# Last layer of a four-layer convolution kernel: tap rows stacked in one product and gathered two chunks later, silu loads moved to GpSimd's queue, distance kept in a buffer of its own, ScalarE's squares put first in each unit

## What the reference computes

```python
patches = _extract_patches(x, KSIZE, STRIDE, PAD)      # 3x3 taps, zero padded
bspl = _b_splines(patches, grid)                       # 8 cubic B-splines of each value
base_w = base_weight.sum(axis=2)
spl_w = (spline_weight * spline_scaler[..., None]).sum(axis=2)
out = jnp.einsum('bjhwn,ijn->bihw', jax.nn.silu(patches), base_w)
out = out + jnp.einsum('bjhwns,ijns->bihw', bspl, spl_w)
out = out + bias_weight[None, :, None, None]
```

## Time and profile before

| | |
|---|---|
| median of three runs | 12108.91 us |
| the profiled execution's own time | 12114.81 us |
| its span | 12112.6 us |
| busy, whole span | PE 79%, DVE 74%, ACT 61%, POOL 42%, weight loads 36% |
| stretch up to the last layer | 0 to 11147 us |
| last layer, loading and norm | 11147 to 11295 us: PE busy 1.14 us, DMA share 0.72 |
| last layer, main loop | 11295 to 12112.6 us: PE 756.88 us, DVE 600.97, ACT 394.12, POOL 307.99 of 817.6; clock 0.96, DMA share 0.45 |

### The profile page before, as it was taken

The page is one execution under the profiler, slowest core; times in us unless marked ns, Lnnn a source line. Parts: engine busy times, 40 slices in busy tenths (PEclk is TensorE's granted clock), DMA queues, the critical chain, the costliest instruction groups (busy, mean ns, idle before and its releaser), DMA issues. The chain is left out here.

```text
span 12112.6 us, 205123 instructions
## 1 busy us (share of the span) xinstructions
PE 9570.5 (79%) x53055; PEld 4412.5 (36%) x53055; DVE 8958.4 (74%) x10913; ACT 7397.5 (61%) x10963; POOL 5088.7 (42%) x2442
## 2 busy tenths in 40 slices
PE   0788578857886788640199999999999999997599
PEld 0566456645664566510022222222222222222233
DVE  1778487847784787637488888888888888887677
ACT  0455345534553455324288888888888888886354
POOL 0233133312321233100166666666666666665243
PEclk9899789977997799875599999999999999999799
DMA  2000100010000000004311111111111111112544
GB/s 86 1 0 0 28 8 0 0 29 7 0 0 21 15 0 0 37 28 143 98 29 29 29 27 25 28 29 29 29 29 29 29 29 27 28 26 54 130 115 100
DMA packets 227136, 410.60 MB, mean 34 GB/s; under 512 B 28784, under 2 KB 163024, under 8 KB 212336
## 3 DMA queue, kind: packets, MB, share of 16 engines
q1 hardware_dynamic: 226150, 399.26, 12.9%
HBM read 283.44 MB, written 115.70 MB: 33 GB/s over the span
## 5 line engine op out<-in xcount | busy, mean ns | idle before, releaser
L1194 POOL TENSOR_TENSOR l_a<-l_a 128x1018 f32<-128x1018 f32 x1851 | 3453.3, 1883 | 1687.8 <-ACT l_a L1339 1673.0
L1309 DVE TENSOR_TENSOR l_r<-l_pps,l_a 128x509 f32<-128x509 f32 x4755 | 2989.0, 677 | 46.0 <-PE l_pps L1208 28.1
L1333 ACT ACTIVATE l_a<-l_qps 128x509 f32<-128x509 f32 x3705 | 2155.3, 596 | 818.4 <-PE l_qps L1208 566.0
L1339 ACT ACTIVATE l_a<-l_a 128x1018 f32<-128x1018 f32 x2380 | 2504.0, 1052 | 40.3 <-issue 40.3
L1208 PE MATMUL l_qps<-l_mv,l_wst 123*128 123x509 bf16 x4235 | 1644.6, 388 | 170.1 <-ACT l_a L1333 50.0
L1208 PE MATMUL l_pps<-l_mv,l_wst 123*128 123x509 bf16 x4228 | 1624.4, 384 | 63.6 <-DVE l_r L1309 60.9
L652 POOL TENSOR_TENSOR a_pr<-a_pr 128x768 f32<-128x768 f32 x384 | 898.4, 2340 | 1639.1 <-DVE a_pr L567 1624.0
L681 ACT ACTIVATE a_g<-a_fps 128x512 f32<-128x512 f32 x1152 | 680.4, 597 | 998.7 <-PE a_fps L434 997.3
L434 PE MATMUL a_fps<-a_hbt,a_wfc 96*128 96x512 f32 x2304 | 1222.2, 666 | 70.2 <-ACT a_g L681 70.2
L452 POOL TENSOR_TENSOR a_pr<-a_qkv 128x768 f32<-128x768 f32 x128 | 386.6, 3039 | 2089.3 <-ACT a_qkv L694 2089.3
L1297 DVE TENSOR_SCALAR l_a<-l_qps 128x509 int32<-128x509 int32 x1058 | 724.5, 685 | 688.2 <-PE l_qps L1208 677.6
(11 more groups left out here) (162 smaller groups left out, 12030.2 us busy)
## 6 DMA issues: line engine op xcount, KB each, us to landing
l_mv<-pw SPq DMA_DIRECT2D x1608, 79.5 KB
l_gx<-g SPq DMA_DIRECT2D x66, 1040.0 KB
pw<-pw_hi SPq DMA_DIRECT2D x165, 127.2 KB
pw<-pw_mid SPq DMA_DIRECT2D x165, 127.2 KB
pw<-pw_lo SPq DMA_DIRECT2D x165, 127.2 KB
a_tb<-g SPq DMA_DIRECT2D x16, 1031.9 KB
l_x<-x SPq DMA_DIRECT2D x16, 1024.0 KB, 12.1
l_gs<-g SPq DMA_DIRECT2D x33, 260.0 KB
```

The costliest lines, as they stand in the source:

```text
L1194: g.tensor_tensor(a, a, a, ALU.mult).then_inc(sq_p, 2)
L1309: v.tensor_tensor(R[:, m % R_RING, :], pps[:, m % P_BANKS, 0:SUB], A[:, m % A_RING, :], ALU.mult).then_inc(mul_done, 1)
L1333: s_.activation(A[:, s % A_RING, :], qps[:, s % Q_BANKS, 0:SUB], ACT.Abs).then_inc(abs_a, 1)
L1339: s_.activation(a, a, ACT.Abs_reciprocal_sqrt, bias=1.0).then_inc(root_done, 2)
```

## The change

Seven things are changed in the last layer; the other layers keep their instructions.

1. The spline products of a chunk no longer read shifted rows. The weights of the three tap rows stand side by side (`wsp`: 3 x 16 columns, padded to 64), so one product gives the contributions of a pixel to three output rows at once, as three "planes". Per image and unit there are three products (the column taps), 24 in a chunk, which go to one PSUM bank per image pair (`pps`, six banks), unit 0 to partitions 0 to 63, unit 1 to 64 to 127.
2. The planes are copied from PSUM to a ring in SBUF (`planes`, three chunks), three of four by ACT and the fourth by DVE (`keep`).
3. `gather(k)` then adds, two chunks later, the planes of three neighbouring rows with 12 small products against a 0/1 matrix (`pick`).
4. The silu is stacked by two: partitions 64 to 127 of `gs` hold the rows one further down, so that one product covers tap rows 0 and 1 and a second one tap row 2. `gs` becomes one buffer of 128 x 1040, filled by six DMAs per chunk that GpSimd issues once the silu before has been taken.
5. The distance goes to a buffer `vb` instead of back to `gx`; `gx` has two buffers instead of three, and is loaded again once the distance has been taken (`v_done`).
6. The slope a is taken on ACT (a Relu, with its sign turned), and the last addition moves from POOL to DVE. POOL does no arithmetic any more.
7. ACT's order in a unit: squares first, then the next unit's distance and slope, then the copies and the silu. `a2` and `b2` have one buffer each. The load of one more small array and a few small DVE and POOL instructions are added ahead of the loop.

```diff
-GX, BSLOTS = 3, 3
+GX, BSLOTS, PSLOTS, PBANKS = 2, 2, 3, 6
+HALF = 2
+KEEP_DVE = {3}
...
                     if n >= GX:
-                        sp.wait_ge(b3_done, n - GX + 1)
+                        sp.wait_ge(v_done, n - GX + 1)
                     src = g3[k, e].rearrange("c j n -> c (j n)").unsqueeze(0).broadcast_to([SPLINE, C, UNIT])
                     sp.dma_start(gx[:, n % GX, :], src).then_inc(gx_in[n % GX], 16)
-                    if e == 0:
-                        if k >= 2:
-                            sp.wait_ge(silu_done, k - 1)
-                        sp.dma_start(gs[:, k % 2, :], g3[k].rearrange("e c j n -> j (e c) n")).then_inc(gs_in[k % 2], 16)
-                    elif k >= 4:
-                        store(k - 4)
+                    if e == 1 and k >= 6:
+                        store(k - 6)
...
+            def silu_after(n):
+                return (n - 3) // PARITY if n >= 3 and n % PARITY else None
+            def kept_after(n):
+                return ((n - 3) // PARITY, (0, 1) if n % PARITY else (2, 3)) if n >= 3 else (None, ())
+            def finished_after(n):
+                return (n - 8) // PARITY if n >= 8 and n % PARITY == 0 and (n - 8) // PARITY < NOUT else None
...
+            @block.gpsimd
+            def _(pool):
+                def load_silu(k):
+                    if k:
+                        pool.wait_ge(silu_done, k)
+                    for h in range(HALF):
+                        rows = g3[k].rearrange("e c j n -> j (e c) n")[2 * h:2 * h + 2]
+                        nc.gpsimd.dma_start(gs[0:64, h, :], rows).then_inc(gs_in, 16)
+                        nc.gpsimd.dma_start(gs[64:P, h, 0:CHN - QW], rows[:, :, QW:]).then_inc(gs_in, 16)
+                        if k + 1 < NCK:
+                            below = g3[k + 1].rearrange("e c j n -> j (e c) n")[2 * h:2 * h + 2, :, 0:QW]
+                            nc.gpsimd.dma_start(gs[64:P, h, CHN - QW:], below).then_inc(gs_in, 16)
...
                 def distance(n):
-                    x = gx[:, n % GX, :]
+                    x = vb[:, n % 2, :]
                     act.wait_ge(gx_in[n % GX], (n // GX + 1) * 16)
-                    s_.activation(x, x, ACT.Abs, bias=place[:], scale=1.0 / GRID_STEP).then_inc(v_done, 1)
+                    if n >= 2:
+                        act.wait_ge(bases, n - 1)
+                    s_.activation(x, gx[:, n % GX, :], ACT.Abs, bias=place[:], scale=1.0 / GRID_STEP).then_inc(v_done, 1)
+                    act.wait_ge(v_done, n + 1)
+                    s_.activation(na[:, n % 2, :], x, ACT.Relu, bias=two[:], scale=-1.0).then_inc(na_done, 1)
...
+                        act.wait_ge(na_done, n + 1)
+                        if n:
+                            act.wait_ge(a3_done, n)
+                        s_.activation(a2[:], na[:, n % 2, :], ACT.Square).then_inc(a2_done, 1)
+                        act.wait_ge(nb_done, n + 1)
+                        if n:
+                            act.wait_ge(b3_done, n)
+                        s_.activation(b2[:], vb[:, n % 2, :], ACT.Square, scale=2.0).then_inc(b2_done, 1)
                     if n + 1 < NUNIT:
                         distance(n + 1)
...
+                        v.tensor_tensor(x, a2[:], x, ALU.mult).then_inc(a3_done, 1)
+                        dve.wait_ge(b2_done, n + 1)
+                        v.tensor_tensor(y, b2[:], y, ALU.mult).then_inc(b3_done, 1)
+                        dve.wait_ge(a3_done, n + 1)
+                        dve.wait_ge(b3_done, n + 1)
+                        if e == 0 and k >= BSLOTS:
+                            dve.wait_ge(plane_made, (k - BSLOTS + 1) * QUAD)
+                        v.tensor_tensor(B[:, e, :, at:at + CHN], y.rearrange("p (j n) -> p j n", j=QUAD),
+                                        x.rearrange("p (j n) -> p j n", j=QUAD), ALU.add).then_inc(bases, 1)
...
+                def multiply(k):
+                    pe.wait_ge(bases, PARITY * (k + 1))
+                    at = k % BSLOTS * CHN
+                    for j in range(QUAD):
+                        m = k * QUAD + j
+                        if m >= PBANKS:
+                            wait_kept(m - PBANKS)
+                        for dx in range(3):
+                            for e in range(PARITY):
+                                x = B[:, e, j, at:at + CHN].rearrange("p (r w) -> p r w", w=QW)[:, :, dx:dx + W]
+                                last = t.matmul(pps[64 * e:64 * e + 64, m % PBANKS, :].rearrange("p (r w) -> p r w", w=W), wsp[:, dx, :],
+                                                x, start=dx == 0, stop=dx == 2, skip_group_check=True)
+                        last.then_inc(plane_made, 1)
...
+                    wait_kept((k + 2) * QUAD - 1)
                     for dy in range(3):
                         for to, n, row in pieces(k, dy):
...
+                            for j in range(QUAD):
+                                last = t.matmul(rows_out[32 * j:32 * j + 32, to:to + n, :], pick[:, dy, :],
+                                                planes[:, j, row:row + n, :], start=False, stop=dy == 2, skip_group_check=True)
                     last.then_inc(o_made, 1)
...
+                for k in range(NCK):
+                    multiply(k)
+                    if k >= 2:
+                        gather(k - 2)
+                gather(NOUT - 1)
```

More of the change, by code:

```diff
@@ new lines, in keep @@
+            def keep(e, copy, k, j):
+                e.wait_ge(plane_made, k * QUAD + j + 1)
+                if k >= PSLOTS:
+                    e.wait_ge(o_made, k - PSLOTS + 1)
+                at = k % PSLOTS * CROWS
+                return copy(planes[:, j, at:at + CROWS, :], pps[:, (k * QUAD + j) % PBANKS, :].rearrange("p (r w) -> p r w", w=W))
+            @block.gpsimd
[11 more added lines that the diff above has]
+                for k in range(NCK):
+                    load_silu(k)
@@ L1545, in _ @@
+                    for j in js:
+                        if j not in KEEP_DVE:
+                            keep(act, lambda to, of: s_.activation(to, of, ACT.Copy), k, j).then_inc(plane_kept, 1)
+                    k = silu_after(n)
+                    if k is not None:
                         silu(k)
@@ L1577, in _ @@
[L1577 to L1591, removed]
+                slope(0)
@@ new lines, in _ @@
+                for n in range(NUNIT + 7):
+                    if n < NUNIT:
+                        k, e = divmod(n, PARITY)
+                        at = k % BSLOTS * CHN
+                        x, y = na[:, n % 2, :], vb[:, n % 2, :]
+                        dve.wait_ge(a2_done, n + 1)
+                        v.tensor_tensor(x, a2[:], x, ALU.mult).then_inc(a3_done, 1)
[7 more added lines that the diff above has]
+                                        x.rearrange("p (j n) -> p j n", j=QUAD), ALU.add).then_inc(bases, 1)
+                    if n + 1 < NUNIT:
+                        slope(n + 1)
+                    k, js = kept_after(n) if n < NUNIT + 3 else (None, ())
+                    for j in js:
+                        if j in KEEP_DVE:
+                            keep(dve, v.tensor_copy, k, j).then_inc(plane_kept_v, 1)
+                    k = finished_after(n)
+                    if k is not None:
+                        finish(k)
@@ L1612, in _ @@
                     pe.wait_ge(silu_done, k + 2)
-                    silu = S[:].rearrange("p k (r w) -> p (k r) w", w=QW)
-                    first = True
+                    silu = S[:].rearrange("p k h (r w) -> p k h r w", w=QW)
+                    for both, dy in ((0, 0), (1, 2)):
+                        for to, n, row in pieces(k, dy):
+                            slots = [(to, n, row)]
+                            if row % CROWS + n > CROWS:
+                                cut = CROWS - row % CROWS
+                                slots = [(to, cut, row), (to + cut, n - cut, row + cut)]
+                            for to_, n_, row_ in slots:
+                                slot, r = divmod(row_, CROWS)
+                                for dx in range(3):
+                                    for h in range(HALF):
+                                        t.matmul(rows_out[64 * h:64 * h + 64, to_:to_ + n_, :],
+                                                 wba[:, both, dx, :, :].rearrange("p b f -> p (b f)"),
+                                                 silu[:, slot, h, r:r + n_, dx:dx + W], start=both == 0 and dx == 0, stop=False,
+                                                 skip_group_check=True)
@@ L1735, in lay_out @@
     got["w3_base"] = np.ascontiguousarray(np.broadcast_to(bw, (NB,) + bw.shape).reshape(P, 9, 9, C))
-    got["w3_mask"] = np.repeat(np.eye(NB, dtype=f32), C, axis=0)
+    got["w3_mask"] = np.tile(np.repeat(np.eye(QUAD, dtype=f32), C, axis=0), (2, 1))
+    planes = np.zeros((2, 4, C, 3, 2, C), f32)
+    for dy in range(3):
+        for e in range(2):
+            planes[e, dy, :, dy, e, :] = np.eye(C)
```

(1 more changed line is left out.)

113 lines of the change are left out of this document (48 added, 65 removed).

## The result

The changed kernel takes 12095.17 us (median of 20 runs, 12052.21 to 12115.38) against 12120.04 us (20 runs) for the one before: ratio 0.9976, 95% interval [0.9966, 0.9986]. It is faster by a quarter of a per cent. I had forecast 12005 us, about 104 us under the kernel before; 25 us came, so three quarters of the gain are missing.

What follows compares the result with a forecast made beforehand. TensorE bounded the old kernel, the loads close behind; afterwards loads bound it at 18.2 + 0.6 + 1.5 = 20.3 us a chunk. 11350.8 + 32.5 P gives 12010.5, corrected to 12005 us for the profiled run's offset; range 11940 to 12080.

Steps and rivals of the forecast that it cites:

- TensorE 18.3 us a chunk: Matrix work in the main loop: 10.4 spline, 5.3 silu, 2.6 gathering if 64-wide products pair; 5.2 us less than before.
- ScalarE 18.1: ScalarE's work in us per main-loop chunk: two units 15.3, PSUM copies 1.8, silu 1.06.
- VectorE's slope: The one slope left on VectorE per unit of the main loop takes 1.24 us.
- The waits between them: Waits among ScalarE, VectorE and TensorE in the main loop cost nothing while a chunk takes above 18 us.
- The `gx` loads as the new bound: In the main loop the loads replace TensorE as bound: 18.2 + 0.6 + 1.5 = 20.3 us a chunk; chance 0.62.
- P: Main-loop period per chunk, forecast 20.3 us; time = 11350.8 + 32.5 P; must be under 23.5 to gain anything.
- the chain of 16.8 us: Next chunk's silu loading, from GpSimd's six issues through landing to the silu: 16.8 us, hidden under 20.3.
- Rival C: Single silu buffer: GpSimd issues up to 3.07 us each make ScalarE wait at its silu; 32.7 us a chunk, 12408; chance 0.08.
- B's cost: Rival: silu loads cost the main loop's gx loads 5.0 us a chunk; 23.8 us, 12118, no change; chance 0.09.
- E: Rival: TensorE idles 2 us a main-loop chunk and its clock falls, costing 1.5 us; 19.8, under 20.3; chance 0.02 in another form.
- The last line of the prediction: Named the main way to be wrong: a silu piece on an engine also carrying gx delays the whole load.
- Faster: Whole kernel's direction: faster than before with chance 0.76, against same 0.11 and slower 0.13.

Runs made afterwards that it cites:

- nosilu: Changed kernel with the silu loads of chunks 1 to 32 left out, output not the reference's: 11953.67 us, ratio 0.9866, loop 654.0 us.
- wide16: Changed kernel with silu pieces put in channel-then-image order, so each uses 16 engines: 11983.8 us, ratio 0.9893, loop 668.1 us.
- gx16: Changed kernel with the gx load spread over 16 engines (channel-then-centre order), silu pieces unchanged: 11947.34 us, ratio 0.9856, loop 647.4 us.
- nogx: Changed kernel with gx loads left out after the first two, units computed from old data: 11964.03 us (one run), loop 653.4 us.
- both16: Changed kernel with both the silu pieces and the gx load on 16 engines: 11942.66 us, ratio 0.9852, loop 646.0 us.

## Why the prediction was wrong, step by step

- TensorE 18.3 us a chunk: right (18.32). ScalarE 18.1: right (17.87 in a chunk without waits). VectorE's slope: right. The waits between them: right; no such wait is left where the loads are out of the way (nosilu).
- The `gx` loads as the new bound: mis-sized. To the 18.2 us of two loads I added 0.6 for the store and 1.5 for the silu. Without the silu two loads and a store fit into TensorE's 18.3 us a chunk (nosilu), and with wide pieces P is 18.9, not 20.3. In the changed kernel the loads are not the bound at all.
- The step that failed: "The silu of the next chunk waits for all six, and they start only when the silu before is done: 6 x 0.6 + 12.1 (landing beside a load) + 1.1 = 16.8 us, hidden under 20.3." The issues cost 0.65 to 0.7 us, about as taken. The landing was the error: 12.1 us was that of one output store behind one load. The silu's six pieces lie on few engines each (two, by the rule in the next item) and meet loads that come without a gap. The last of them took up to 26.5 us to land, and the chain of 16.8 us took 30 in the long cases (11580.92 to 11611.12). In about every second chunk it was longer than the chunk; that is 125.7 us of waits, and P = 22.2 instead of 18.3.
- I had the rule of the two engines beside this and drew the wrong conclusion from it. The Trainium skill, DMA: Bandwidth & Descriptors, section "Why a DMA increments its semaphore by 16 and not by 1", gives two engines for a piece whose slowest dimension is 2. I used it for what the silu costs the load, not for what the load costs the silu. With the slowest dimension at 32 (wide16) or the load's at 16 (gx16) the waits were all but gone (5.1 and 3.4 us), as by that rule.
- Rival C named the place (ScalarE at its silu, behind it the squares and copies) with the wrong price: the issue, not the landing. B's cost was not found. E happened in a small way: TensorE stood idle for 2.25 us ahead of the silu's products at 11612.34, and from 11612 to 11616 its mean clock was 0.57, near the lower level of 0.50 (1.2 GHz), where the four microseconds before had 1.00. Over the whole stretch the clock was 0.93. It came after the stalls and did not set the time: TensorE waited for the splines next.
- The last line of the prediction was the mirror image of what happened: I feared that a silu piece on one of the load's engines would delay the load, and it was the load that delayed the piece.
- Faster was right as a direction; the size was not.

What stays open: the loop is 43.5 us shorter in the traces, the medians differ by 25. The profiled execution of the kernel before was 5 us under its median, and the number of long waits can differ from run to run; I did not separate these. How two queues take turns on an engine was not measured: the trace does not say on which engine a packet ran. That `gx` beside the pieces is the cause is shown (nogx, gx16), and so is that the pieces' own width matters (wide16); the turn-taking is argued. GpSimd's pauses between issues have no releaser in the trace.

## What to carry to other kernels

When a load moves to a single buffer, compare the next use with its worst landing beside the traffic that will be there, not with a median of another transfer, and count the engines it is spread over. The DMA share at 0.48 did not mean room: with one load in flight it was 0.49, half of the engines were full, and an eight-fold repeat on the outside of the access pattern was the reason. Swapping the repeat with the channels was worth 126 us of the loop here (773.8 to 647.4), but only after TensorE's work had shrunk; before that it was worth nothing.

## What the hardware showed that I had not expected

- The same 1040 KB load ran at 117 GB/s with eight repeats outside, and with 16 channels outside at 248 GB/s while it had the engines to itself.
- Chunks of about 31 us and of 17.9 us follow each other by themselves: a stall drains the loads, and so the next silu pieces come quickly.
- GpSimd pauses at fixed places. In the traces with narrow pieces and a `gs` of one buffer (the changed kernel, nogx and gx16) it stood still ahead of its 32nd, 63rd, 94th, 125th and 156th issue, every 31 issues, for 5.0 to 12.2 us in the changed kernel (three of these pauses fall into long waits) and 4.6 to 7.8 us in the other two. With wide pieces it did so once, ahead of the 129th issue, for 11.7 us (wide16) and 3.8 us (both16). No run here shows what it waits for.
